# A two-layer transformer block on one core: a finer first attention and a later last recurrence

## The chip, the core and the metric

The kernel runs on one core of a Trainium2 chip. The core has five engines with an instruction list each: TensorE (PE) for products, VectorE (DVE) for elementwise work, reductions and scans, ScalarE (ACT) for functions and copies with a scale, GpSimd (POOL), here mostly for issuing transfers that add into SBUF, and SyncE (SP) for plain transfers. A list is worked off strictly in order; engines wait for each other by semaphores. The metric is the device time of one execution in microseconds, lower is better.

## The reference

Two layers, each of an attention and a feed-forward part, on `x` of shape (4, 256, 256), that is 4 batches of 256 tokens and 256 channels. Each of the four parts is fed not with `x` itself but with `x` gated by a bidirectional recurrence over `fside`:

```python
decay = exp(-exp(w)) * (0.5 + 0.5 * tf);  ek = exp(min(kf, 30));  ekv = ek * vf
# forwards and backwards over time: a = a * decay + ekv_t;  b = b * decay + ek_t
num = nf + nb - ekv + exp(min(u + kf, 30)) * vf
den = df + db - ek + exp(min(u + kf, 30))
out = sigmoid(r) * num / max(den, 1e-8) * (0.8 + 0.2 * tf)      # r is x
```

First attention: `w = x @ W.T` in 16 heads of 16; `q`, `k`, `v` are `w` normalised by its root mean square in each head, times the gains `g1`, `g2`, `g3`. The weights are `softmax(att, -1) + softmax(att, -2)`, and the output goes through `W`. First feed-forward: one product with both sides in 8 bits, scaled by the largest value of the whole input. Second attention: `q`, `k` rotated by position, blocks masked causally, softmax over rows. Second feed-forward: two products with ternary weights and activations rounded to 8 bits, a squared ReLU between them. After each part `x = x + part`.

## The kernel before

The recurrences are independent of `x`, so they are run ahead. There are 16, numbered `n = 4 * part + batch`. Each needs, in this order: `prepare(n)` on ACT (two exponentials and the decay tile), `inputs(n)` on DVE, two forward scans `ahead(n, 0)` and `ahead(n, 1)`, two backward scans `behind(n, 0)` and `behind(n, 1)`, the adding transfers `add_mid(n)` and `add_back(n)` issued by POOL, `wkv(n)` on ACT (a logarithm and an exponential, which give the reciprocal), and `gate(n)` on DVE. Then `gated(part, batch)` multiplies the gate with `1 + tanh(x / 2)` of `tanh(part, batch)`. Recurrence 0 is summed by DVE itself (`summed`).

The first attention is written as 38 slots `p`, eight for each batch (`b, j = divmod(p, 8)`), two heads a slot. In each slot every engine's list holds its share of: scores of slot `p` (`scores0`), their exponential (L486), every second slot the values (`values0`), copy and turn of their rows (`rows_copy`, `turn_rows`), the division `links` on DVE, which also yields scaled values for the column softmax, and the column product (`columns0`). For the next batch a slot holds in turn: projection `project0` (j = 1), `square0` and `sums0` (2), `rms` (3), `normed` (4), transposes of the rows by `turn` (5), `kT_copy` (6) and `low_parts` (7), which split keys and queries into two half-precision parts. `v_rows` on POOL multiplies the values with `g3`. Behind comes the output of the batch before: `turn_y`, `yT_copy`, `turned_copy`, `project_both`, `residual`. Recurrence `n` from 3 on is placed by `M_AT[n] = 3 * (n - 3)`: `prepare` one slot before, `inputs` at it, scans one and two behind, `wkv` five, `gate` six.

After the slots come the tail with recurrence 15's scans, `wkv(13)` and `wkv(14)`, the largest value, the 8-bit product and its scaled copy (L515), bias and sum (L840, L842), `gated(2, 0)`.

The second attention has slots from -16 (`SLOTS1`). At slots -16, -8, 0, 8 it holds `gated(2, b)`, `project_qk` (L1139) and the rotation `rotary`, then `project_v` and POOL's additions (L338), the turns of q and k (L996), copies, `maxima` on PE and `negmax` (L865) on DVE 11 slots ahead of their use, a second turn of q with the maxima in it, and from slot 0 on `scores1`. `wkv(LAST)` stands at slot -4, its gate at 0. PSUM tile `PM` of two banks serves all projections and turns.

## Time and profile before

| | us |
|---|---|
| median of 3 runs | 414.3 (413.16 to 419.51) |
| the profiled execution | 414.29 |
| its span | 412.5 |
| PE busy in it | 270.0 (65%) |
| DVE busy | 264.5 (64%) |
| ACT busy | 203.1 (49%) |
| POOL busy | 53.9 (13%) |

The span is the part that the profiler records on the core. Busy shares are means over stages that have different limits, so none of them says by itself what an edit is worth.

### The profile page before, as it was taken

How to read it: one execution, taken by the hardware profiler on the slowest of the kernel's cores; microseconds unless marked ns; L12 is line 12 of the kernel's file. 1: busy time of each engine (PE TensorE's matmuls, PEld its weight loads, DVE VectorE, ACT ScalarE, POOL GpSimd, SP SyncE). 2: the span in 40 equal slices, each digit the busy share in tenths (PEclk: the TensorE clock that was granted, in tenths of full speed). 3: DMA queues.
4: the chain of work that ended last, by engine and by line, in shares of the span. 5: the costliest groups of instructions: out<-in, count | busy, mean ns of one | idle time of the engine just before them, and what ended most of it. 6: DMA issues, size and time to landing. Idle time of an engine off the chain costs nothing.

```text
span 412.5 us, 5473 instructions
## 1 busy us (share of the span) xinstructions
PE 270.0 (65%) x2054; PEld 165.7 (40%) x2054; DVE 264.5 (64%) x494; ACT 203.1 (49%) x326; POOL 53.9 (13%) x79
## 2 busy tenths in 40 slices
PE   0031564769388498683266867789899899665644
PEld 0020422436145245252132444546666666334413
DVE  4695996987688786799743746373464230694762
ACT  4744369574775854648212272734542533143521
POOL 3012031131013022121330203020000000000000
PEclk9975589598598778867585859998965955966986
DMA  7825255264266355455200000000000000000100
GB/s 202 318 52 102 51 104 102 52 117 88 52 172 126 61 104 114 91 102 102 53 0 0 0 2 0 2 0 2 2 1 2 0 2 0 2 0 0 52 27 25
DMA packets 8522, 23.55 MB, mean 57 GB/s; under 512 B 1584, under 2 KB 2992, under 8 KB 8112
## 3 DMA queue, kind: packets, MB, share of 16 engines
q0 software_dynamic: 4320, 15.73, 20.2%
q1 hardware_dynamic: 4176, 7.48, 5.4%
...
## 4 chain that ended last, share of the span: by engine, by line
PE 41%; DVE 24%; ACT 17%; issue 9%; DMA 5%; SPq 1%; POOL 1%; DVEq 0%; ACTq 0%; POOLq 0%
PE PS L1191 8%; PE PM L1139 5%; PE PM L996 4%; PE PO L1206 3%; DVE fwd L639 3%; PE PO L1042 3%; PE PO L1027 3%; PE PM L1082 3%; PE PM L1068 2%; DVE fwd L910 2%; DMA fwd<-bwd 2%; DVE bwd L647 2%; PE PO L1270 2%; DMA fwd<-mid 2%; ACT E L486 2%
## 5 line engine op out<-in xcount | busy, mean ns | idle before, releaser
L865 DVE TENSOR_REDUCE kp<-PS 128x2 f32<-128x256 f32 x64 | 32.3, 553 | 34.6 <-PE PS L1170 34.6
L486 ACT ACTIVATE E<-PS,negc,escale 128x1024 f32<-128x1024 f32 x32 | 38.3, 1199 | 15.1 <-PE PS L1010 15.1
L554 ACT ACTIVATE E<-PS 128x384 f32<-128x384 f32 x64 | 27.9, 490 | 35.0 <-PE PS L1191 35.0
L1042 PE MATMUL PO<-E,vr 128*32 128x256 f32 x256 | 23.7, 502 | 22.2 <-DVE vr L748 16.4
L1010 PE MATMUL PS<-TP 32*128 32x256 f16 x256 | 21.8, 303 | 22.5 <-DVE TP L689 22.5
L996 PE MATMUL PM<-ident,kp 128*128 128x128 f32 x128 | 21.6, 323 | 11.1 <-DVE kp L677 6.4
L1139 PE MATMUL PM<-G,sg 128*128 128x512 f32 x32 | 20.8, 809 | 9.4 <-DVE sg L662 9.3
L984 PE MATMUL PM<-w,sg 128*128 128x256 f32 x32 | 11.2, 511 | 23.2 <-DVE sg L662 23.2
L458 ACT ACTIVATE yc<-PO 128x256 f32<-128x256 f32 x32 | 12.4, 386 | 25.6 <-PE PO L1027 24.2
L267 POOL DMA_DIRECT2D fwd<-mid x15 | 13.8, 918 | 85.5 <-DVE fwd L639 85.5
L1010 PEld LDWEIGHTS PS<-TP 32*128 32x128 f16 x256 | 10.7, 101 | 33.8 <-DVE TP L689 23.6
L1191 PE MATMUL PS<-TP 32*128 32x128 f32 (+1 forms) x128 | 20.4, 419 | 5.7 <-ACT E L554 3.2
L1027 PE MATMUL PO<-E,vt 128*32 128x256 f32 x256 | 23.7, 501 | 0.0
L996 PEld LDWEIGHTS PM<-ident,kp 128*128 128x128 f32 x128 | 17.1, 165 | 14.8 <-issue 8.3
L1191 PE MATMUL PS<-w,TP 32*128 32x256 f32 (+1 forms) x128 | 20.4, 428 | 2.6 <-ACT E L554 2.5
...
L1042 PEld LDWEIGHTS PO<-E,vr 128*32 128x32 f32 x256 | 8.2, 128 | 31.2 <-DVE vr L748 22.4
L639 DVE TENSOR_TENSOR_SCAN fwd<-DT,ekv 128x512 f32<-128x512 f32 x16 | 20.3, 1267 | 0.0
L647 DVE TENSOR_TENSOR_SCAN bwd<-ekv,DT 128x511 f32<-128x511 f32 x16 | 20.2, 1262 | 0.0
L1191 PEld LDWEIGHTS PS<-TP 32*128 32x128 f32 x128 | 15.2, 230 | 12.0 <-ACT E L554 4.4
L639 DVE TENSOR_TENSOR_SCAN fwd<-DT,ek 128x512 f32<-128x512 f32 x16 | 19.5, 1217 | 0.0
L386 ACT ACTIVATE fwd<-fwd,lnmin 128x512 f32<-128x512 f32 x16 | 11.5, 721 | 15.9 <-DMA fwd<-bwd 15.9
...
## 6 DMA issues: line engine op xcount, KB each, us to landing
fwd<-mid POOLq DMA_DIRECT2D x15, 512.0 KB, 4.6
fwd<-bwd POOLq DMA_DIRECT2D x15, 512.0 KB, 4.5
...
w<-in_attn SPq DMA_DIRECT2D x1, 512.0 KB, 7.1
```

The costliest lines, as they stand in the source:

```text
L267: nc.gpsimd.dma_start(fwd[:, r], mid[:, o], accum_op=ALU.add).then_inc(S[f"mid_added{o}"], 16)
L486: nc.scalar.activation(E[:, p % 6], PS[:, 2 * (p % 2):2 * (p % 2) + 2, :], ACT.Exp, bias=negc[:], scale=escale[:]).then_inc(S["e0_done"], 1)
L554: nc.scalar.activation(E[:, p % 4, i, 0:384], PS[:, i, 0:384], ACT.Exp, scale=QSCALE).then_inc(S["e1_done"], 1)
L639: nc.vector.tensor_tensor_scan(fwd[:, r, i], DT[n % 2][:, 0:SEG], src[:, seg(b)], 0.0, ALU.mult, ALU.add).then_inc(S["scan_done"], 1)
L647: nc.vector.tensor_tensor_scan(bwd[:, n % 2, i, 0:SEG - 1][:, ::-1], src[:, seg(b, 1, SEG - 1)][:, ::-1], DT[n % 2][:, 1:SEG][:, ::-1], 0. ...
L865: nc.vector.tensor_reduce(kp[:, b % 2, u * H + 2 * j:u * H + 2 * j + 2, D], PS[:, at0:at0 + 2, lo:hi], AX, ALU.max, negate=True).then_inc( ...
L996: ins = nc.tensor.transpose(PM[:, c // 2, at:at + P], src.rearrange("p g s -> p (g s)"), ident[:])
L1010: ins = nc.tensor.matmul(PS[:, 2 * (p % 2) + i, u * T:(u + 1) * T], khl[b % 2][r:r + SLOT, c, u * P:(u + 1) * P], q[b % 2][r:r + SLOT, c, ...
L1027: ins = nc.tensor.matmul(PO[SLOT * g:SLOT * (g + 1), 0, 0:T], vt[:, b % 2, v * H + 4 * c + g, :], E[:, (2 * q + g // 2) % 6, g % 2, v * T: ...
L1042: ins = nc.tensor.matmul(PO[SLOT * g:SLOT * (g + 1), 1, at:at + T], vr[:, q % 2, v * 4 + g, :], E[:, (2 * q + g // 2) % 6, g % 2, v * T:(v ...
L1139: ins = nc.tensor.matmul(PM[:, u, :], sg[:, seg(b, k * T + u * P, P)], w1a[:, k, 0:2, :].rearrange("p n c -> p (n c)"), start=(k == 0), st ...
L1191: ins = nc.tensor.matmul(PS[:, i, 2 * v * P:2 * P + v * P], k[r:r + ROWS, c, v * P:(v + 1) * P], q[r:r + ROWS, c, v * P:2 * P], start=True ...
```

## The change

- Key chain in halves. The transposes of a batch (`turn`) become `turn0(b, k)`: half `k` (two of the four head groups) in slots 5 and 6, with `kT_copy(b, k)` and `low_parts(b, k)` in halves as well; `scores0` waits for the half that it reads. A transpose of 128 columns becomes four products with 32 columns each.
- Values in place. `normed` writes both copies of a row into a wider tile `kv`, whose third part holds ones; `values0` and `links` read the values there. `v_rows` and its semaphore go. `g3` is applied in the scale of `yT_copy` and `turned_copy`.
- First logarithm moved up. Loads are reordered (`x` first), all four `tanh(0, s)` stand behind `prepare(0)`, and `wkv(0)` stands before `prepare(1)`.
- Recurrences: `n = 2` leaves the head for slot 0, so that 2 to 11 are spread over slots 0 to 33, `n = 12` takes the place of 15 in the tail, and 13 to 15 go to the slots -15 to -2 of the second attention, with `wkv(12)` and `gate(12)` at the first of them.
- Order in a slot: on ACT `wkv` stands behind the exponential and the copies, on DVE `residual` stands first and `low_parts` behind the scans. `gated(2, 0)` and its tanh stand behind the second residual sum of the feed-forward; the weight steps move by one slot.

```diff
-        kp = sb("kp", [P, 2, 2 * TT * H, SLOT])
+        kpf = sb("kp", [P, 2 * 2 * TT * H * SLOT])
+        kp = kpf[:].rearrange("p (n r s) -> p n r s", n=2, s=SLOT)
+        WIDE = 3 * D
+        kv = kpf[:, 0:2 * TT * H * WIDE].rearrange("p (n r s) -> p n r s", n=2, s=WIDE)
...
-        RAMP = 3
+        RAMP = 2
+        BEFORE = 3 * LAYERS
         LAST = LAYERS * B - 1
-        M_AT = {n: 3 * (n - RAMP) for n in range(RAMP, LAYERS * B)}
-
+        M_AT = {n: 3 * (n - RAMP) for n in range(RAMP, BEFORE)}
+        M_AT[BEFORE] = B * PAIRS + 4
+        M_LATE = {BEFORE + i: -17 + 3 * i for i in range(1, B)}
+
+        def steps1(p, lag):
+            return [n for n, at in M_LATE.items() if at + lag == p]
...
-            sp.dma_start(xT[:, seg(0)], xT_d[:, seg(0)]).then_inc(S["ld_x0"], 16)
+            for b in range(2):
+                sp.dma_start(xT[:, seg(b)], xT_d[:, seg(b)]).then_inc(S[f"ld_x{b}"], 16)
+            sp.dma_start(gcol[:], gcol_d).then_inc(S["ld_gcol"], 16)
+            sp.dma_start(gains[:], gains_d.partition_broadcast(P)).then_inc(S["ld_gains"], 16)
             sp.dma_start(kT[:, seg(1)], kT_d[:, seg(1)]).then_inc(S["ld_k1"], 16)
-            sp.dma_start(w0[:], attn0_d).then_inc(S["ld_attn0"], 16)
-            sp.dma_start(kT[:, seg(2)], kT_d[:, seg(2)]).then_inc(S["ld_k2"], 16)
-            sp.dma_start(gains[:], gains_d.partition_broadcast(P)).then_inc(S["ld_gains"], 16)
-            sp.dma_start(gcol[:], gcol_d).then_inc(S["ld_gcol"], 16)
-            sp.dma_start(ident[:], ident_d).then_inc(S["ld_ident"], 16)
-            sp.dma_start(xT[:, seg(1)], xT_d[:, seg(1)]).then_inc(S["ld_x1"], 16)
-            sp.dma_start(kT[:, seg(3)], kT_d[:, seg(3)]).then_inc(S["ld_k3"], 16)
             for b in range(2, B):
                 sp.dma_start(xT[:, seg(b)], xT_d[:, seg(b)]).then_inc(S[f"ld_x{b}"], 16)
+            sp.dma_start(w0[:], attn0_d).then_inc(S["ld_attn0"], 16)
+            sp.dma_start(ident[:], ident_d).then_inc(S["ld_ident"], 16)
+            for b in range(2, B):
+                sp.dma_start(kT[:, seg(b)], kT_d[:, seg(b)]).then_inc(S[f"ld_k{b}"], 16)
...
-            def v_rows(b):
-
-                pool.wait_ge(S["k0_done"], b + 1)
-                if b >= 2:
-                    pool.wait_ge(S["pv0_done"], CH * (b - 1))
-                nc.gpsimd.tensor_tensor(vt[:, b % 2, :, 0:D], kp[:, b % 2, 0:TT * H, 0:D],
-                                        gains[:, 2, None, :].broadcast_to([P, TT * H, D]),
-                                        ALU.mult).then_inc(S["v0_done"], 1)
...
+            nc.gpsimd.memset(kv[:, :, :, 2 * D:WIDE], 1.0).then_inc(S["pads_set"], 1)
...
+            add_mid(1)
+            add_back(1)
+            for p in range(SLOTS0):
+                for n in steps0(p, 1):
+                    if n < BEFORE:
+                        add_mid(n)
+                for n in steps0(p, 2):
+                    if n < BEFORE:
+                        add_back(n)
+            add_mid(BEFORE)
+
+
+            pool.wait_ge(S["ktr0_done"], HALF * B)
+            pool.wait_ge(S["y0_done"], B * CH)
             nc.gpsimd.memset(vt[:, :, :, D:2 * D], 1.0).then_inc(S["v_ones"], 1)
...
+            add_back(BEFORE)
             for p in SLOTS1:
                 b, j = p // PAIRS + 2, p % PAIRS
+                for n in steps1(p, 1):
+                    add_mid(n)
+                for n in steps1(p, 2):
+                    add_back(n)
...
+                    for s in range(B):
+                        tanh(0, s)
                 if b == 1:
-                    tanh(0, 0)
-            prepare(1)
-            for b in range(1, B):
-                tanh(0, b)
-            nc.scalar.preload_act_table_set("natural_log_exp_and_others")
-            act.wait_ge(S["ln_bias"], 1)
-            wkv(0)
-            prepare(2)
+                    nc.scalar.preload_act_table_set("natural_log_exp_and_others")
+                    act.wait_ge(S["ln_bias"], 1)
+                    wkv(0)
+                    prepare(1)
...
-            def kT_copy(b):
-                act.wait_ge(S["ktr0_done"], b + 1)
+            def kT_copy(b, k):
+                act.wait_ge(S["ktr0_done"], HALF * b + k + 1)
                 if b >= 2:
-                    act.wait_ge(S["qk0_done"], PAIRS * (b - 1))
-                rows = PM[:].rearrange("p k (c t) -> p (k c) t", t=T)
-                nc.scalar.activation(khigh[b % 2], rows, ACT.Copy).then_inc(S["kT0_done"], 1)
-                nc.scalar.activation(qhigh[b % 2], rows, ACT.Copy, scale=gq[:]).then_inc(S["kT0_done"], 1)
-
-            def yT_copy(b, turned, used, done):
+                    act.wait_ge(S["qk0_done"], PAIRS * (b - 2) + 4 * k + 4)
+                rows = PM[:, k, :].rearrange("p (c t) -> p c t", t=T)
+                nc.scalar.activation(khigh[b % 2][:, 2 * k:2 * k + 2], rows, ACT.Copy).then_inc(S["kT0_done"], 1)
+                nc.scalar.activation(qhigh[b % 2][:, 2 * k:2 * k + 2], rows, ACT.Copy,
+                                     scale=gq[:]).then_inc(S["kT0_done"], 1)
...
             square0(0)
+            prepare(2)
+            rms(0)
             weight_abs(0)
-            rms(0)
-            weight_abs(1)
             act.wait_ge(S["gains_done"], 1)
-            wkv(1)
-            kT_copy(0)
-            prepare(3)
+            for k in range(HALF):
+                kT_copy(0, k)
             for p in range(SLOTS0):
                 b, j = divmod(p, PAIRS)
-                if p == 2:
-                    wkv(2)
-                for n in steps0(p, 5):
-                    if n <= 12:
-                        wkv(n)
                 if p < B * PAIRS:
...
-                if p % 2 == 0 and 0 <= p // 2 - 1 < B * CH:
-                    rows_copy(p // 2 - 1, 0, "pv0_done", "turned0_done", "rows0_done")
-                if j == 2 and b + 1 < B:
+                if p == 0:
+                    wkv(1)
+                    weight_abs(1)
+                if j == 1 and b + 1 < B:
                     square0(b + 1)
                 if j == 3 and b + 1 < B:
                     rms(b + 1)
+                if p % 2 == 0 and 0 <= p // 2 - 1 < B * CH:
+                    rows_copy(p // 2 - 1, 0, "pv0_done", "turned0_done", "rows0_done")
                 if j == 3 and 1 <= b <= B:
-                    yT_copy(b - 1, "ytr0_done", "out0_done", "yT0_done")
+                    yT_copy(b - 1, "ytr0_done", "out0_done", "yT0_done", gv[:])
+                if j == 5 and b + 1 < B:
+                    kT_copy(b + 1, 0)
+                if j == 6 and b + 1 < B:
+                    kT_copy(b + 1, 1)
                 if p % 4 == 3 and p >= 7 and (p - 7) // 4 < B * HALF:
                     turned_copy((p - 7) // 4)
-                if j == 6 and b + 1 < B:
-                    kT_copy(b + 1)
+                for n in steps0(p, 5):
+                    if n < BEFORE:
+                        wkv(n)
                 for n in steps0(p, -1):
                     if n > RAMP:
                         prepare(n)
-                if p in (5, 13):
-                    weight_round(1 - (p - 5) // 8)
+                if p in (4, 12):
+                    weight_round(1 - (p - 4) // 8)
                 if p == 33:
                     for bb in range(B - 1):
                         tanh(1, bb)
 
 
             tanh(1, B - 1)
-            for n in range(13, LAST):
-                wkv(n)
             for b in range(B):
                 act.wait_ge(S["ffn0_done"], b + 1)
                 nc.scalar.activation(y8[:, b], PS[:, b, :], ACT.Copy, scale=sc8[:, 5:6]).then_inc(S["y8_done"], 1)
+                if b == 1:
+                    tanh(2, 0)
 
...
-                if p == -4:
-                    wkv(LAST)
+                for n in steps1(p, -1):
+                    prepare(n)
+                if steps1(p, 5):
+                    nc.scalar.preload_act_table_set("natural_log_exp_and_others")
+                for n in steps1(p, 5):
+                    if n == BEFORE + 1:
+                        wkv(BEFORE)
+                    wkv(n)
...
             inputs(1)
+            sums0(0)
             ahead(1, 0)
+            normed(0)
             ahead(1, 1)
-            sums0(0)
             behind(1, 0)
+            low_parts(0, 0)
             behind(1, 1)
-            normed(0)
-            inputs(2)
-            ahead(2, 0)
-            ahead(2, 1)
-            low_parts(0)
-            behind(2, 0)
-            behind(2, 1)
-            gate(1)
+            low_parts(0, 1)
...
-                if j == 0 and b + 1 < B:
-                    gated(0, b + 1)
+                if j == 5 and 1 <= b <= B:
+                    residual("out0_done", b, 0, b - 1)
                 if j == 4 and b + 1 < B:
                     normed(b + 1)
-                if j == 7 and b + 1 < B:
-                    low_parts(b + 1)
-                if p == 3:
-                    gate(2)
-                for n in steps0(p, 6):
-                    if n <= 12:
-                        gate(n)
-                if p == SLOTS0 - 2:
-                    for bb in range(B - 1):
-                        gated(1, bb)
-                        largest(bb)
                 for n in steps0(p, 0):
                     inputs(n)
                 for n in steps0(p, 1):
-                    if n < LAST:
+                    if n < BEFORE:
                         ahead(n, 0)
                         ahead(n, 1)
                 for n in steps0(p, 2):
-                    behind(n, 0)
-                    behind(n, 1)
-                if j == 5 and 1 <= b <= B:
-                    residual("out0_done", b, 0, b - 1)
+                    if n < BEFORE:
+                        behind(n, 0)
+                        behind(n, 1)
+                if p == 0:
+                    gate(1)
+                for n in steps0(p, 6):
+                    if n < BEFORE:
+                        gate(n)
+                if j == 0 and b + 1 < B:
+                    gated(0, b + 1)
+                if j == 6 and b + 1 < B:
+                    low_parts(b + 1, 0)
+                if j == 7 and b + 1 < B:
+                    low_parts(b + 1, 1)
                 if p % 2 == 1 and 0 <= (p - 3) // 2 < B * CH:
                     links((p - 3) // 2)
                 if j == 2 and b + 1 < B:
                     sums0(b + 1)
+                if p == 34:
+                    for bb in range(B - 1):
+                        gated(1, bb)
+                        largest(bb)
                 if p == 1:
...
-            behind(LAST, 0)
-            behind(LAST, 1)
+            behind(BEFORE, 0)
             for b in range(B):
                 dve.wait_ge(S["y8_done"], b + 1)
...
                 nc.vector.tensor_tensor(xT[:, seg(b)], xT[:, seg(b)], y8[:, b], ALU.add).then_inc(S["x_done"], 1)
+                if b == 1:
+                    gated(2, 0)
+            behind(BEFORE, 1)
...
-                if p in (-15, -13, 0):
-                    gate(13 + (p + 15) // 2 if p < 0 else LAST)
+                for n in steps1(p, 6):
+                    if n == BEFORE + 1:
+                        gate(BEFORE)
+                    gate(n)
+                for n in steps1(p, 0):
+                    inputs(n)
+                for n in steps1(p, 1):
+                    ahead(n, 0)
+                    ahead(n, 1)
+                for n in steps1(p, 2):
+                    behind(n, 0)
...
+            def turn0(b, k):
+                if k == 0:
+                    pe.wait_ge(S["k0_done"], b + 1)
+                elif b >= 2:
+                    pe.wait_ge(S["x_done"], b - 1)
+                for c in (2 * k, 2 * k + 1):
+                    for u in range(TT):
+                        at = (c % 2) * T + u * P
+                        for g in range(4):
+                            ins = nc.tensor.matmul(PM[SLOT * g:SLOT * (g + 1), k, at:at + P],
+                                                   kv[:, b % 2, u * H + 4 * c + g, 0:SLOT], ident[:],
+                                                   start=True, stop=True)
+                ins.then_inc(S["ktr0_done"], 1)
...
                 if j == 5 and b + 1 < B:
-                    turn(b + 1, 0, "ktr0_done", [("k0_done", b + 2)] + ([("x_done", b)] if b >= 1 else []))
+                    turn0(b + 1, 0)
+                if j == 6 and b + 1 < B:
+                    turn0(b + 1, 1)
```

## Rows read from the trace of the kernel before

**Rows 1.** Stretches: start:end us, length, busy us (instructions) by engine, granted clock, DMA share, GB/s.

```profile
74.29:110.19 35.90, 25.14 (x236) 14.73 (x236) 27.95 (x41) 22.79 (x34) 7.29 (x7) 0.79 0.47 89
...
167.70:189.85 22.15, 12.77 (x72) 7.39 (x72) 19.83 (x31) 12.18 (x21) 3.44 (x4) 0.77 0.50 95
...
204.13:243.25 39.12, 27.20 (x117) 14.68 (x117) 19.19 (x37) 12.52 (x15) 6.72 (x10) 0.67 0.00 0
243.25:412.50 169.25, 131.79 (x972) 86.22 (x972) 81.39 (x209) 65.67 (x121) 6.16 (x9) 0.79 0.02 7
```

**Rows 2.** Head, timeline: start, length, engine, line, tiles, count, [idle before <-releaser].

```profile
18.69 0.69 DVE L613 SCALAR_TENSOR_TENSOR G<-fwd 128x512 f32<-128x512 f32 x1 [3.04 <-ACT fwd L388]
...
20.23 3.46 PE L984 MATMUL PM<-w,sg 128*128 128x256 f32 x8 [20.23 <-DVE sg L662]
...
36.73 0.72 ACT L386 ACTIVATE fwd<-fwd,lnmin 128x512 f32<-128x512 f32 x1 [7.66 <-DMA fwd<-bwd]
...
42.60 1.07 PE L1010 MATMUL PS<-TP 32*128 32x256 f16 x16 [10.53 <-DVE TP L689]
...
51.56 1.21 ACT L486 ACTIVATE E<-PS,negc,escale 128x1024 f32<-128x1024 f32 x1 [0.30 <-PE PS L1010]
```

**Rows 3.** The page's table of groups: busy us and mean ns of one, idle before.

```profile
L865 DVE TENSOR_REDUCE kp<-PS 128x2 f32<-128x256 f32 x64 | 32.3, 553 | 34.6 <-PE PS L1170 34.6
...
L639 DVE TENSOR_TENSOR_SCAN fwd<-DT,ekv 128x512 f32<-128x512 f32 x16 | 20.3, 1267 | 0.0
...
L386 ACT ACTIVATE fwd<-fwd,lnmin 128x512 f32<-128x512 f32 x16 | 11.5, 721 | 15.9 <-DMA fwd<-bwd 15.9
```

**Rows 4.** First attention, timeline.

```profile
57.97 1.93 PE L1042 MATMUL PO<-E,vr 128*32 128x256 f32 x16 [3.89 <-DVE vr L748]
...
60.36 2.24 DVE L639 TENSOR_TENSOR_SCAN fwd<-DT,ekv 128x512 f32<-128x512 f32 x1
...
83.45 1.07 PE L1042 MATMUL PO<-E,vr 128*32 128x256 f32 x16
...
106.58 1.28 DVE L687 SCALAR_TENSOR_TENSOR TP<-TP,gcol,PM 128x1024 f16<-128x1024 f16 x1 [4.35 <-ACT TP L444]
...
163.40 0.69 DVE L694 TENSOR_TENSOR xT<-PM,xT 128x512 f32<-128x512 f32 x1 [3.41 <-PE PM L1082]
...
174.80 0.43 DVE L626 TENSOR_SCALAR mid<-mid 128x512 f32<-128x512 f32 x1 [1.90 <-ACT mid L369]
```

**Rows 5.** The page's DMA issues: median us from issue to landing, last.

```profile
fwd<-mid POOLq DMA_DIRECT2D x15, 512.0 KB, 4.6
fwd<-bwd POOLq DMA_DIRECT2D x15, 512.0 KB, 4.5
```

**Rows 6.** End of the first attention and first feed-forward, timeline.

```profile
186.49 0.68 DVE L694 TENSOR_TENSOR xT<-PM,xT 128x512 f32<-128x512 f32 x1
...
192.29 3.57 PE L1124 MATMUL PS<-E,w8q 128*128 128x256 fp8e4 x16 [1.94 <-DVE E L833]
...
195.70 2.40 ACT L515 ACTIVATE E<-PS,cond 128x512 bf16<-128x512 f32 x4
...
203.39 0.68 DVE L662 SCALAR_TENSOR_TENSOR sg<-sg,G 128x512 f32<-128x512 f32 x1
```

**Rows 7.** From 204.13 us to the second attention, timeline.

```profile
211.60 0.60 ACT L564 ACTIVATE vt<-PM 128x512 f32<-128x512 f32 x1 [12.98 <-PE PM L1148]
...
219.68 0.63 ACT L359 ACTIVATE sg<-xT 128x512 f32<-128x512 f32 x1
...
223.01 6.18 PE L1139 MATMUL PM<-G,sg 128*128 128x512 f32 x8 [1.03 <-DVE sg L662]
...
230.91 1.41 POOL L338 TENSOR_TENSOR kp<-G 128x256 f32<-128x256 f32 x2 [0.92 <-DVE G L854]
...
232.38 1.10 PE L996 MATMUL PM<-ident,kp 128*128 128x128 f32 x8 [0.22 <-POOL kp L338]
...
238.32 1.28 ACT L386 ACT_TABLE_LOAD   x1
```

88 lines of the change are left out of this document (37 added, 51 removed).

## The prediction

> **What bounds the kernel now.** I first cut the span into stages by the table of stretches [rows 1], then read each stage in order of time for who waits for whom. The table of groups gives the price of one operation. No engine is full anywhere: in the first attention the VectorE (DVE) is busy 27.95 of 35.90 us per batch and the TensorE (PE) 25.14, between the attentions DVE is busy 19.19 of 39.12. What costs time is that each engine runs its own list in order, and a list stands still whenever its head waits. So I don't compare sums of work. I carry the new lists through, with the durations of the rows, and note when each list is at the same point. "Slot" is the index of the written order, S(n) a pair of scans of recurrence n, log(n) the two ScalarE (ACT) operations of `wkv(n)`.
>
> Three places matter. The head: the first scores start at 42.60, after PE idled 10.53 [rows 2], and one ScalarE operation on 512 columns costs 0.72 there [rows 3]. The first attention: DVE idles 4.35 at the low parts of the keys, which comes once a batch, and 3.41 at a residual [rows 4]. The stretch 204.13 to 243.25, from the projection of q and k of batch 0 to the first scores of the second attention [rows 1]: a chain PE, DVE, GpSimd (POOL), PE, ACT, DVE in which every engine idles and none may be late.
>
> **Head.** DVE waits 3.04 us for log(0) [rows 2]. In the new order ACT has log(0) done before the numerator is summed, so the gate starts 3.0 earlier and the projection at 17.2 instead of 20.23. It ends at 20.7 (3.46 us, [rows 2]). Then square 0.6, head sums 0.65, an interposed `prepare(2)` of 1.5 (two exponentials of 256 columns and a copy of 510, two and a half times the 0.6 to 0.7 of 512 columns, [rows 3]), root 0.55: 23.4. Two normalising operations 1.25, first half of the turn 1.8, two copies of 512 columns 1.1, two low parts 1.3: first scores near 29, 13.5 earlier. The full-width turn before took 1.94 with PE at 1.2 GHz; the new one is 16 products per half, 32 columns wide. Its nearest row is the column product: 8 such products (16 instructions) with 256 moving columns, four to side-by-side quarters of the output, show as 1.93 at 1.2 GHz and 1.07 at 2.4 [rows 4]. 16 products with 128 columns move as many columns, so I take the same, 1.0 to 1.9. Bounds per half: below, the old turn's 1.94 for both halves, 0.5 each at 2.4 GHz; above, if the four don't overlap, four times 1.93, 7.7.
>
> Most is not kept. After exponential 0, ACT has log(1), which needs the second accumulating transfer: S ends at 25.8 and 30.1, the transfers take 4.6 and 4.5 to land [rows 5] plus 0.5 to start, so log(1) starts at 35.4, behind it stand the sum of the second weight and exponential 1 (39), gate 1, the gating of batch 1 and its projection (38.2 to 41.9). Exponential 2 comes at 43.5, against 51.56 [rows 2]: **-8.1**.
>
> **Slots 2 to 31.** Density of recurrences is the same, one per three slots, one index behind. Gone: the POOL multiplication for the values, beside which a scan of 1.2 took 2.24 [rows 4]; one wait of 4 us per batch shrinks because half 0 of the keys is ready when DVE gets there. New: the inputs of n wait on DVE for `prepare(n)`, which stands behind log, copies and exponential on ACT. This wait exists now (1.90 before the inputs at 174.80, [rows 4]); in my walk it is 2.5 to 3 at slots 6, 9, 15 and more at 18. Also new: the residual is first in its slot instead of behind the scans, so DVE stands before it for 3 us while scans could run (now: 3.41, in one batch only, [rows 4]). And logs move behind the exponential of their slot, which takes the transfer's wait off the exponentials. Checkpoints of the walk, against now: exponential 8 -11.6, 16 -10.3, 24 -7.8. I enter **-2** for this stage (bounds +4 and -8).
>
> **Slots 28 to 38.** Recurrences 13 and 14 leave, and 12 shrinks to its inputs and one scan: 18 us of DVE work (6.3 per recurrence: four scans, 1.13 apart in order of time though 1.22 each [rows 3], inputs 0.43 + 0.7 [rows 4], gate 0.69 [rows 2]). I credit only **-1**. The 22.15 us after the last exponential [rows 1] are bound by exponential, columns, values, copy, turn, and PE's two projections; DVE's work lay in their gaps. It was late at the end only for the last residual, which stands behind the inputs of 15 and starts at 186.49 [rows 6]; PE was done about 1 us before. In front of the links of the last quarter the new order even puts gate 11, which waits for log(11).
>
> **First feed-forward.** Products start at 192.29, the first scaled copy only at 195.70, since log(13) and log(14) with four table loads lie before it [rows 6]: -2.5. The gating of batch 0 moves from behind all four residual sums (203.39, [rows 6]) to behind the second: two sums of some 1.2 (estimate: two operations of 0.3 and one of 0.7) and a scan of 1.13, which moves behind them, less what POOL's clearing of `kp` (now right behind transfer 12) blocks of the first sum: -2.3. Together **-4.8**. The scan behind and two sums fit under PE's 3.8 us until the first rotation. So the projection starts at 204.1 - 8.1 - 2 - 1 - 4.8 = 188.
>
> **The stretch to the second attention.** Times from that start; now it ends at 39.1 [rows 1]. Recurrences 13, 14, 15 enter.
> (a) ACT: the copy of v ends at 8.1 [rows 7], `prepare(13)` 9.6; DVE inputs 10.2, S(13) ahead 12.45. POOL 0.5, transfer 4.8 to the next issue, second one 4.5: log(13) can start at 22.3. Behind it in ACT's list is the tanh of batch 1, which now starts at 15.6 (219.68, [rows 7]). 22.3 + log 1.35 + table load 1.28 + tanh 0.63 + gating 0.7 = 26.3, and q, k of batch 1 are projected then, instead of 18.9: **+7.4**. DVE, with three maxima and four scans, is ready at about the same time, so both would have to be faster.
> (b) POOL: the list puts transfer 15 ahead of the rotary additions of batch 1. It needs S(15) ahead, and this stands behind both rotations. From the projection's start: rotations done 7.8, two gates 1.25, inputs 1.1, a pair of maxima 1.0 (0.55 each, [rows 3]), scans 2.3, issue 0.5 + 0.9, additions twice 1.4 [rows 7], clearing 0.15: turn of q at 17.9, now 9.4 (223.01 to 232.38, [rows 7]): **+8.5**.
> (c) Turn of q to first scores, now 10.9: log(15) with two loads, 4.0 from 238.32 [rows 7], goes from in front of the copy of q. Enter: turn and copy 2.2, load and log(14) 2.6, gate 14 0.6 in front of maxima 6 and 7 (1.9), turn 2.0, copy 1.0, log(15) 2.6 (1.35 if the set, still loaded, isn't loaded again), gate 15 0.6 in front of maxima 9 and 10 (1.9), for which the first scores wait: 15.5. **+4.6**.
> Gate 15 is gone from the second attention, -0.6. Sum +19.9; bounds: +12, if the waits of (c) fall into the lag of (b) and the third load is absent, and +24.
>
> The Trainium skill speaks against this placement (ScalarE: Activation LUTs, What ACT_TABLE_LOAD costs): it puts a switch of set at about 2.66 us, drain included. The load here takes 1.28 [rows 7]. By the page three switches on the chain would add some 4 us to the sum.
>
> **Sum.** The rest, 169.25 us [rows 1], has the same lists and stays. 412.5 - 16 + 20 = 416.5 of span; the profiled execution took 414.29, 1.8 more than its span and equal to the median of 414.3. Forecast **418**. Its own range is 411 to 424.
>
> **Rivals.** (1) The first attention is bound by DVE after all. Then what leaves counts in full: 18.7 us, and the contention of 3, on top of the head. For it: DVE is busy 78% of the batch [rows 1], more than any other. Against it: PE has 70%, in other places of the slot, and each waits for the other. The projection would start 27 earlier instead of 16: 407. (2) The stretch absorbs the recurrences, as DVE is idle for 19.93 of 39.12 there. Then only the excess of DVE's list over the chain stays, about 6: 404. Against it: (a) is a transfer latency and (b) an order on one queue; neither asks how idle DVE is. (3) Slower: DVE's stands in front of the residual. At slots 13, 21 and 29 the residual waits for PE's projection; now the scans run in that wait. If each of the three costs its full 3.3 on the links behind it, the first part gains only 6: 426.5 + 1.8 = 428. It decides if the links of slots 13, 21, 29 come over 2.6 us after the residual; a pair of scans stands between only at 29, which speaks against the full price. (4) The head doesn't move: x of batches 2 and 3 now load before the second key segment and ACT's tanh of them stands before log(0). If they land after 12.7, log(0) is as late as now: 3 back, 421.
>
> **Chances.** Forecast 0.47, (1) 0.15, (2) 0.13, (3) 0.20, (4) 0.05. A measurement of this kernel tells 2% from no change, 406.0 and 422.6. Faster: (2) and a third of (1), with some of my walk's own error, 0.20. Slower: (3) and the upper end of the forecast, 0.27. Range 403 to 427: from under (2) to just short of (3), where the ends of the unknown costs (-24 + 12 and -8 + 24 on the span) lie as well.
>
> **What would show it.** First scores near 29 and exponential 2 near 43.5; an ACT wait of some 4 us before log(1). Exponentials 8, 16, 24 at -11, -10, -8. Start of the q, k projection near 188. Then table load, log(13), load, tanh in ACT's order with a wait on the transfer, 26 us from that start to the second projection; POOL's additions of batch 1 behind a transfer issue; DVE waiting for ACT before gates 14 and 15; some 59 us to the first scores. Wrong if the stretch is under 50, or if the projection starts before 180.

## The result, and the profile after

The changed kernel takes **429.75 us** (median of 3 runs, 429.28 to 430.33) against 414.3: ratio 1.0388, 95% interval 1.0343 to 1.0434. The forecast was 418.0, range 403 to 427: right in sign, 11.75 us short, and outside the range. The profiled execution is that of the median: 429.75, span 428.0, mean granted clock 0.780.

I put the marks of the two traces side by side, each the start of the same work, and beside them the mark of the forecast.

| us | before | forecast | after |
|---|---|---|---|
| exponential 2 | 51.56 | 43.5 | 46.48 |
| exponential 24 | 142.9 | 135.1 | 135.5 |
| exponential 31 | 167.7 | | 164.6 |
| 8-bit quantisation | 191.65 | | 185.40 |
| 8-bit products | 192.29 | | 189.69 |
| projection q, k of batch 0 | 204.13 | 188 | 195.01 |
| of batch 1, from there | +18.9 | +26.3 | +26.50 |
| turn of q of batch 1, from there | +9.4 | +17.9 | +18.83 |
| first scores, from there | +10.9 | +15.5 | +16.82 |
| end, from there | 169.25 | 168.65 | 170.8 |

By its terms the forecast's span ends at 416.4 (188 + 59.7 + 168.65). Of the 11.6 us that it is longer, 7.0 are there when the projection starts, 2.4 come in the stretch and 2.2 behind the first scores. The table of stretches has the same three places (start:end, length, busy us of PE, weight load, DVE, ACT, POOL, granted clock, DMA share, GB/s); its rows answer to [rows 1]:

```profile
63.70:101.50 37.80, 25.17 (x292) 15.08 (x292) 29.39 (x46) 24.64 (x39) 5.15 (x6) 0.82 0.42 79
164.60:185.40 20.80, 11.61 (x74) 7.35 (x74) 12.31 (x26) 9.13 (x15) 0.13 (x1) 0.83 0.01 1
195.01:257.16 62.15, 28.47 (x117) 15.83 (x117) 40.59 (x65) 25.14 (x33) 13.14 (x18) 0.61 0.31 59
257.16:427.90 170.74, 132.66 (x972) 86.53 (x972) 80.55 (x208) 65.24 (x120) 5.79 (x9) 0.79 0.02 7
```

DVE's work in the stretch between the attentions doubles, 19.19 to 40.59, while its length grows by 23.0.

**Head.** ACT's timeline, answering to [rows 2]:

```profile
7.22 0.21 ACT L398 ACTIVATE ew<-vec 128x8 f32<-128x8 f32 x1 [1.92 <-DMA vec<-in_vec]
...
38.54 0.72 ACT L389 ACTIVATE fwd<-fwd,lnmin 128x512 f32<-128x512 f32 x1 [4.52 <-DMA fwd<-bwd]
...
46.48 1.20 ACT L482 ACTIVATE E<-PS,negc,escale 128x1024 f32<-128x1024 f32 x1 [0.56 <-PE PS L1042]
```

The wait in front of log(1) is there, 4.52 for "some 4". The first scores start at 32.15 (forecast: near 29). Everything is shifted: the first small load is used at 7.22, in before's trace at 4.76.

**Last batch of the first attention.** DVE's timeline:

```profile
150.87 1.20 DVE L649 TENSOR_TENSOR_SCAN fwd<-DT,ekv 128x512 f32<-128x512 f32 x1
157.29 0.69 DVE L704 TENSOR_TENSOR xT<-PM,xT 128x512 f32<-128x512 f32 x1 [5.21 <-PE PM L1112]
157.89 1.21 DVE L657 TENSOR_TENSOR_SCAN bwd<-ek,DT 128x511 f32<-128x511 f32 x1
159.02 1.20 DVE L657 TENSOR_TENSOR_SCAN bwd<-ekv,DT 128x511 f32<-128x511 f32 x1
160.13 0.18 DVE L744 RECIPROCAL rrec<-PO 128x8 f32<-128x8 f32 x1
```

The two scans behind the residual don't need it. They stand still with it for 5.21 us, and the links (the reciprocal) come behind both, 2.84 behind the residual. At slots 13 and 21 it is much the same: waits of 3.49 and 3.53 us, and the links 2.86 and 2.33 behind. On the page the residual's row (8 of them, four in the first attention) has the idle time in front:

```profile
L704 DVE TENSOR_TENSOR xT<-PM,xT 128x512 f32<-128x512 f32 x8 | 5.5, 690 | 26.9 <-PE PM L1112 15.0
```

The 15.0 us are the four of the first attention (3.49, 3.53, 5.21, 2.74); in the trace before they are 5.6.

**First feed-forward.** DVE, then POOL, then the 8-bit products on PE:

```profile
185.40 5.36 DVE L839 TENSOR_SCALAR E<-sg,cond 128x512 fp8e4<-128x512 f32 x4
```

```profile
185.27 0.86 POOL L276 DMA_DIRECT2D fwd<-mid  x1 [23.64 <-DVE fwd L649]
185.80 1.71 POOL L316 MEMSET vt<- 128x1536 f32 x1
187.12 2.14 POOL L319 MEMSET kp<- 128x2048 f32 x1
```

```profile
189.69 3.57 PE L1157 MATMUL PS<-E,w8q 128*128 128x256 fp8e4 x16 [5.60 <-DVE E L839]
```

Four quantisations took 1.68 in all before; they take 5.36 here, of which the first alone has 4.15: it ends at 189.55, just behind the large fills (189.26). The products wait for it and start 4.29 us behind its start, 0.64 before. In the trace before, the fill of `kp` lay beside the second pair of bias sums, which took 2.60 instead of 0.61:

```profile
197.65 2.60 DVE L840 TENSOR_SCALAR E<-E,bias 128x256 bf16<-128x256 bf16 x2
...
197.71 2.14 POOL L321 MEMSET kp<- 128x2048 f32 x1
```

**The stretch.** Logarithm 13 on ACT, which waits for its transfer until 22.4 from the start (forecast 22.3) and stands ahead of the tanh of batch 1; POOL's issue of transfer 15 ahead of the additions; and DVE's two waits for gates:

```profile
217.41 0.72 ACT L389 ACTIVATE fwd<-fwd,lnmin 128x512 f32<-128x512 f32 x1 [0.69 <-DMA fwd<-bwd]
...
220.11 0.63 ACT L362 ACTIVATE sg<-xT 128x512 f32<-128x512 f32 x1
```

```profile
235.31 0.86 POOL L276 DMA_DIRECT2D fwd<-mid  x1 [13.79 <-DVE fwd L649]
...
236.42 3.86 POOL L341 TENSOR_TENSOR kp<-G 128x256 f32<-128x256 f32 x4
```

```profile
246.09 0.69 DVE L623 SCALAR_TENSOR_TENSOR G<-fwd 128x512 f32<-128x512 f32 x1 [6.77 <-ACT fwd L391]
...
254.46 0.69 DVE L623 SCALAR_TENSOR_TENSOR G<-fwd 128x512 f32<-128x512 f32 x1 [4.88 <-ACT fwd L391]
```

### The profile page after: what moved, and what is told of

Read it like the earlier page. It is cut to its first block, busy times and chain, and to the rows that moved or that the text cites. A ratio compares the mean times of both kernels' runs of the same rounds, so it can differ in the third digit from the quotient of the medians.

```text
span 428.0 us, 5935 instructions
## 1 busy us (share of the span) xinstructions
PE 275.2 (64%) x2278; PEld 170.7 (40%) x2278; DVE 262.7 (61%) x502; ACT 204.8 (48%) x333; POOL 47.1 (11%) x76
## 4 chain that ended last, share of the span: by engine, by line
PE 44%; DVE 27%; ACT 12%; issue 10%; DMA 4%; POOL 2%; DVEq 0%; ACTq 0%; POOLq 0%
PE PS L1224 7%; DVE fwd L649 5%; PE PO L1072 5%; PE PM L1172 4%; PE PM L1112 4%; PE PO L1057 4%; PE PO L1239 3%; PE PM L1028 3%; PE PM L1098 2%; DVE fwd L918 2%; DMA fwd<-mid 2%; DMA fwd<-bwd 2%; DVE bwd L657 2%; PE PM L1181 2%; DVE kp L873 2%
## 5 line engine op out<-in xcount | busy, mean ns | idle before, releaser
L873 DVE TENSOR_REDUCE kp<-PS 128x2 f32<-128x256 f32 x64 | 32.3, 551 | 25.5 <-PE PS L1203 25.4
L482 ACT ACTIVATE E<-PS,negc,escale 128x1024 f32<-128x1024 f32 x32 | 38.3, 1198 | 11.6 <-PE PS L1042 11.4
L1072 PE MATMUL PO<-E,vr 128*32 128x256 f32 x256 | 22.7, 483 | 32.7 <-DVE vr L751 26.4
L460 ACT ACTIVATE yc<-PO 128x256 f32<-128x256 f32 x32 | 12.4, 387 | 30.5 <-PE PO L1057 29.1
L1224 PE MATMUL PS<-TP 32*128 32x256 f32 (+1 forms) x128 | 20.2, 417 | 9.3 <-DVE kp L873 6.0
L1172 PE MATMUL PM<-G,sg 128*128 128x512 f32 x32 | 21.8, 842 | 6.6 <-DVE sg L672 6.5
L1028 PE MATMUL PM<-ident,kp 128*128 128x128 f32 x96 | 17.5, 341 | 10.9 <-POOL kp L341 8.8
L1057 PE MATMUL PO<-E,kp 128*32 128x256 f32 x256 | 23.2, 494 | 0.0
L623 DVE SCALAR_TENSOR_TENSOR G<-fwd 128x512 f32<-128x512 f32 x16 | 10.9, 686 | 18.5 <-ACT fwd L391 18.3
L1203 PE MATMUL PS<-E 32*128 32x128 bf16 (+1 forms) x128 | 12.1, 292 | 15.5 <-DVE kp L873 14.4
L704 DVE TENSOR_TENSOR xT<-PM,xT 128x512 f32<-128x512 f32 x8 | 5.5, 690 | 26.9 <-PE PM L1112 15.0
L1002 PEld LDWEIGHTS PM<-w,sg 128*128 128x128 f32 x32 | 7.9, 261 | 30.1 <-DVE sg L672 28.7
```

The costliest lines, as they stand in the source:

```text
L482: nc.scalar.activation(E[:, p % 6], PS[:, 2 * (p % 2):2 * (p % 2) + 2, :], ACT.Exp, bias=negc[:], scale=escale[:]).then_inc(S["e0_done"], 1)
L873: nc.vector.tensor_reduce(kp[:, b % 2, u * H + 2 * j:u * H + 2 * j + 2, D], PS[:, at0:at0 + 2, lo:hi], AX, ALU.max, negate=True).then_inc( ...
L1002: ins = nc.tensor.matmul(PM[:, 0, u * C:(u + 1) * C], sg[:, seg(b, k * T + u * P, P)], w0[:, 0, k, :], start=(k == 0), stop=(k == HALF - 1))
L1028: ins = nc.tensor.transpose(PM[:, c // 2, at:at + P], src.rearrange("p g s -> p (g s)"), ident[:])
L1057: ins = nc.tensor.matmul(PO[SLOT * g:SLOT * (g + 1), 0, 0:T], kv[:, b % 2, v * H + 4 * c + g, D:WIDE], E[:, (2 * q + g // 2) % 6, g % 2, v ...
L1072: ins = nc.tensor.matmul(PO[SLOT * g:SLOT * (g + 1), 1, at:at + T], vr[:, q % 2, v * 4 + g, :], E[:, (2 * q + g // 2) % 6, g % 2, v * T:(v ...
```

## The experiments

Sixteen kernels ran in four groups, each group on one chip beside runs of the kernel before (414.71, 414.54, 414.63 and 416.09 us there). "Projection" below is the start of q, k of batch 0, "rest" the time from the first scores to the end of the span, "clock" the granted TensorE clock. The medians of the kernel before differ by up to 1.5 us between the groups, so small differences across groups are better read from the ratios. The first small load is issued at 1.65 in every trace, but is used at 4.50 to 5.03 in the four traces without late recurrences (before, e7, e9, e13) and at 5.78 to 7.22 in the fourteen with them. Marks of two traces can differ by up to 2.7 us from that alone, and why it goes with the kernel, the runs don't show.

### The two halves of the change

**e4, the kernel before with recurrences 13 to 15 moved to the second attention, and nothing else.**

```
-        M_AT = {n: 3 * (n - RAMP) for n in range(RAMP, LAYERS * B)}
+        BEFORE = 3 * LAYERS
+        M_AT = {n: 3 * (n - RAMP) for n in range(RAMP, BEFORE)}
+        M_AT[BEFORE] = B * PAIRS + 4
+        M_LATE = {BEFORE + i: -17 + 3 * i for i in range(1, B)}
...
```

> The kernel before with the late recurrences alone: 12 in the tail, 13 to 15 in the slots before the second attention, as in the changed kernel; head, keys, values and orders of the first attention as before. If the late placement is the loss, the stretch is 60 to 62 us instead of 39 and the end of the first attention gains 2 to 5: before plus 17 to 21, 431 to 435 us. If the loss is in the finer first attention, the time is near 414 to 418.

429.72 us, ratio 1.0381 (1.033 to 1.0431): the whole loss comes with them alone. Their logarithms, gates, scans and transfers stand as in the changed kernel. The quantisation starts at 184.91 instead of 191.65 though the last exponential isn't earlier (168.3), so the recurrences that leave free 7.3 us between the two, where I had entered 1. The stretch takes 63.4 us instead of 39.1.

**e7, the changed first attention with all 16 recurrences in it.**

```
-        M_AT[BEFORE] = B * PAIRS + 4
-        M_LATE = {BEFORE + i: -17 + 3 * i for i in range(1, B)}
+        M_AT[13], M_AT[14], M_AT[LAST] = 32, 34, B * PAIRS + 4
...
```

> The changed first attention (keys in halves, values in place, logarithm and loads moved) with all 16 recurrences in it and their logarithms and gates placed as before; 13 to 15 start at slots 32, 34 and 36. No recurrence in the second attention. Theory A (all of the loss is the late recurrences, +15 us by the run of before with them alone, and the first attention's own changes are worth about nothing): 413 to 416, projection of q and k at 203 to 206. Rival (the head's 8 to 11 us are real and are kept until the end of the first attention when VectorE's list is short enough): projection at 196 to 199 and 406 to 409 us.

412.54 us, ratio 0.9945 (0.9899 to 0.9992). Here the first load was used at 4.50, and exponential 2 came at 43.3, where the forecast had it. The projection starts at 199.04, 5.1 earlier than before: less than half of the 11.9 by which exponential 16 is (98.3 against 110.2). The time lies between the two that I had expected to choose from. The first attention's own change is worth 0.5%, and late recurrences on top of it cost 17.2.

### The end of the first attention

**e12, the residual behind the scans of its slot again.**

```
-                if j == 5 and 1 <= b <= B:
-                    residual("out0_done", b, 0, b - 1)
...
+                if j == 5 and 1 <= b <= B:
+                    residual("out0_done", b, 0, b - 1)
                 if p % 2 == 1 and 0 <= (p - 3) // 2 < B * CH:
                     links((p - 3) // 2)
```

> The changed kernel with one part undone: the residual of the first attention stands behind the scans of its slot again, in front of the links. Rival (3) of my prediction said that the residual in front lets VectorE wait with scans behind it; the trace has that wait, 5.21 us at 157.29. If it costs: the last exponential comes 2 to 4 us earlier and the time is 426 to 428. If not (the links have time): within 0.7 us of 429.75.

421.10 us (419.73 to 422.37), **8.65 less** than the changed kernel and more than expected; ratio to before 1.0162 (1.0093 to 1.023). DVE's timeline at the same place:

```profile
148.21 1.19 DVE L657 TENSOR_TENSOR_SCAN bwd<-ek,DT 128x511 f32<-128x511 f32 x1
149.32 1.19 DVE L657 TENSOR_TENSOR_SCAN bwd<-ekv,DT 128x511 f32<-128x511 f32 x1
153.51 0.69 DVE L704 TENSOR_TENSOR xT<-PM,xT 128x512 f32<-128x512 f32 x1 [3.00 <-PE PM L1112]
154.43 0.21 DVE L744 RECIPROCAL rrec<-PO 128x8 f32<-128x8 f32 x1 [0.22 <-PE PO L1081]
```

The scans run in the wait, and the links come 0.92 behind the residual instead of 2.84. That is 1.9 us of order at this place. The four waits of the first attention come to 5.4 us instead of 15.0. The table of stretches, from exponential 24 to 31 and on to the quantisation, of the changed kernel and then of e12, shows where more of it lies:

```profile
135.50:164.60 29.10, 23.93 (x211) 12.53 (x204) 15.54 (x25) 14.37 (x21) 4.09 (x5) 0.73 0.48 91
```

```profile
133.60:157.80 24.20, 20.45 (x194) 11.19 (x186) 15.44 (x25) 14.15 (x21) 3.44 (x4) 0.79 0.58 110
157.80:177.07 19.27, 10.30 (x74) 6.29 (x74) 12.31 (x26) 9.14 (x16) 0.13 (x1) 0.85 0.00 1
```

The first stretch is 4.9 us shorter. Of that, 1.9 lie already between exponentials 24 and 25 (139.90 less 135.52, against 136.06 less 133.62), where no residual stands; PE waits longer there for the links and its next two groups of products take longer. The changed kernel, then e12:

```profile
135.25 1.93 PE L1072 MATMUL PO<-E,vr 128*32 128x256 f32 x16 [3.37 <-DVE vr L751]
...
136.95 1.93 PE L1057 MATMUL PO<-E,kp 128*32 128x256 f32 x16
```

```profile
132.49 1.07 PE L1072 MATMUL PO<-E,vr 128*32 128x256 f32 x16 [2.60 <-DVE vr L751]
...
133.38 1.66 PE L1057 MATMUL PO<-E,kp 128*32 128x256 f32 x16
```

The other 3.0 lie between exponentials 29 and 31, around the residual. The clock is granted at 0.79 instead of 0.73, and at 0.85 instead of 0.83 behind the last exponential; the two projections there took 5.8 us (3.78 and 2.19, overlapping) in the changed kernel and 3.7 (1.99 and 1.89) in e12, the same 16 products. This is no accident of one run: of the kernels with the residual in front, eleven traces have 29.1 to 30.1 us from exponential 24 to 31, and e8 has 28.0; with it behind the scans it is 23.6 to 25.5 in e12, e13, e14, e15 and in both kernels of the old order (before, e4). So the order costs, and a lower clock comes with it (0.9 us between these two traces are the head's). How the 8.65 divide between the two, and whether the clock follows from the order alone, the runs don't separate.

**e6, POOL's clearing moved.**

```
             nc.gpsimd.memset(kv[:, :, :, 2 * D:WIDE], 1.0).then_inc(S["pads_set"], 1)
+            nc.gpsimd.memset(vt[:, :, :, D:2 * D], 1.0).then_inc(S["v_ones"], 1)
...
             pool.wait_ge(S["y0_done"], B * CH)
-            nc.gpsimd.memset(vt[:, :, :, D:2 * D], 1.0).then_inc(S["v_ones"], 1)
+            pool.wait_ge(S["xq8_done"], B)
```

> The changed kernel with only GpSimd's clearing moved: the ones beside the values of the second attention are set at the start, and kp is cleared after the four 8-bit quantisations instead of beside them. Theory A (the clearing stretches the quantisation, which took 5.36 us instead of 1.68): the quantisation takes 1.7 again, the 8-bit products and the projection of q and k start 3.7 earlier, and the time falls by 3 to 4 us to about 426. Rival (the clearing costs the same wherever it lies, since VectorE's bias sums are then stretched): the products start 3.7 earlier, the projection by under 1, and the time stays within 1 us of 429.7.

425.09 us (422.93 to 425.51), **4.7 less**; ratio to before 1.0249 (1.0178 to 1.032). DVE, then POOL:

```profile
184.15 1.68 DVE L840 TENSOR_SCALAR E<-sg,cond 128x512 fp8e4<-128x512 f32 x4
...
186.87 1.31 DVE L846 TENSOR_SCALAR E<-E,bias 128x256 bf16<-128x256 bf16 x2
```

```profile
185.97 1.81 POOL L320 MEMSET kp<- 128x2048 f32 x1 [0.86 <-DVE E L840]
```

The quantisation is back at 1.68, 3.7 less, and 2.95 of that arrive at the projection: the interval from quantisation to projection falls from 9.61 to 6.66. The other 0.7 go to the first pair of bias sums, beside which the fill now lies: 1.31 instead of 0.58. (The projection itself is 4.2 earlier, 1.2 of it from the head.)

**e8, the two halves of the keys handled together.**

```
-                if j == 5 and b + 1 < B:
+                if j == 6 and b + 1 < B:
                     turn0(b + 1, 0)
...
```

ACT's copies of half 0 go from 5 to 6 and DVE's low parts from 6 to 7.

> The changed kernel with one part undone: in the loop of the first attention the two halves of the keys are turned, copied and split together at the slots of the second half (6, 6 and 7), as a whole. Theory A (halving takes one wait of some 4 us per batch down, as my prediction had it within its -2): exponentials 8, 16 and 24 later by 1 to 3 each, in all 2 to 5 us at the projection, 432 to 434 us. Rival (the halves gain nothing, since PE and VectorE wait elsewhere in the slot): exponentials within 0.5 us of the changed kernel, 429 to 431 us.

429.76 us, equal to the changed kernel, where I had expected 432 to 434 if the halves were worth anything. Exponentials 8 and 16 come 2.8 and 2.2 later (66.5, 103.7), 24 is 1.8 later, 31 only 0.7, and the projection 0.7. The halves work as described, and their gain is given back before the attention ends.

### The stretch

**e1, POOL's additions of batch 1 ahead of the transfers.**

```
             for p in SLOTS1:
-                for n in steps1(p, 1):
-                    add_mid(n)
-                for n in steps1(p, 2):
-                    add_back(n)
...
                                                     ALU.add).then_inc(S["qkp_done"], 1)
+                for n in steps1(p, 1):
+                    add_mid(n)
+                for n in steps1(p, 2):
+                    add_back(n)
```

> The changed kernel (429.75 us) with one order altered: on GpSimd the rotary additions of batch 1 stand ahead of the issue of recurrence 15's first transfer. If the additions' place in that queue is a link of the chain, the turn of q of batch 1 starts some 9 us after its projection instead of 18.8, and, as VectorE then still has scans and a gate ahead of maxima 6 and 7, the stretch to the second attention shrinks from 62 to 52 to 55 us: 420 to 423 us. If the stretch is bound by VectorE's own list (recurrences 13 to 15 and the gates in it), less than 2 us are gained: 428 to 430.

423.11 us (421.18 to 425.14), **6.6 less**; the turn of q of batch 1 is 13.0 behind its projection instead of 18.8, and the stretch is 56.0, a little more than the 52 to 55 expected.

**e2, gates 12 and 13 at slot -8, gates 14 and 15 at slot 3 of the second attention.**

```
-                for n in steps1(p, 6):
-                    if n == BEFORE + 1:
-                        gate(BEFORE)
-                    gate(n)
+                if p == -8:
+                    gate(BEFORE)
+                    gate(BEFORE + 1)
...
+                if p == 3:
+                    gate(BEFORE + 2)
+                    gate(BEFORE + 3)
```

> The changed kernel with gates 14 and 15 behind slot 3 of the second attention instead of slots -5 and -2. The changed trace shows VectorE idle 6.8 us before gate 14 and 4.9 before gate 15. If these stands are the cost, the first scores come 5.6 earlier and the first exponential, which stands behind log 15 and a tanh on ScalarE, 3 earlier: 426 to 427.5 us. If the maxima behind gate 14 wait for the turn of q anyway and those behind gate 15 for ScalarE's logarithm in another way, nothing changes: 429 to 430.

Three executions took 429.34 to 430.69 and one 416.21, with the granted clock at 0.761 to 0.780 and 0.826, so no ratio is given. The profiled one, of clock 0.761, has the stretch 4.7 shorter (57.4) and the rest 4.4 longer (175.3). With such a spread neither expectation is settled.

**e3, both, and the logarithms moved**: 12 and 13 behind the tanh of batch 1, 14 and 15 to slot 2.

```
-                if steps1(p, 5):
+                if p in (-8, 2):
                     nc.scalar.preload_act_table_set("natural_log_exp_and_others")
...
```

> The changed kernel with the stretch reordered as a whole: additions first on GpSimd, logs 12 and 13 behind the tanh of batch 1, logs 14 and 15 at slot 2, gates 14 and 15 at slot 3. If the recurrences cost time there only by where they stand in the lists, the stretch falls from 62 to some 45 us and the kernel to 411 to 415. If VectorE's added 19 us of work or the transfers bound the stretch, it stays at 52 or more: 420 us or more.

421.22 us (419.06 to 423.47), ratio 1.0162 (1.0116 to 1.0208). The stretch falls to 48.4, 7.6 under e1, and only 1.9 of that are in the time: the rest takes 178.25 instead of 170.8. The stretch came near the 45 expected, the time (411 to 415) didn't.

### All together

**e9 and e13: e7 with e6's clearing, then with e12's residual besides.**

> As the kernel with the changed first attention alone (e7), and GpSimd's clearing moved as in e6. Theory A: 3 to 4 us under e7, so about 410 to 412. Rival: equal to e7.

> No late recurrences: the changed first attention alone (e7) with the clearing moved (e9) and the residual behind the scans (e12). If all three add up: 412.5 less 3 to 5 less 0 to 3, so 406 to 410 and faster than before by 1 to 2%. Rival (the first attention gives a shift of its own back in the granted clock, as e9 did against e7): 411 to 413.

e9: 412.02 us, four executions from 403.76 to 415.37 with clocks of 0.773 to 0.834; its exponential 31 came 3.0 later than in e7, and the gain of the clearing can't be read from it. e13: **408.17 us** (402.82 to 408.5), ratio 0.9829 (0.9751 to 0.9907). This is the version that beats both kernels: the new first attention, the old stage for the recurrences, the old place of the residual, and the clearing behind the quantisation.

**e10, e11, e14, e15: the late recurrences kept, mended.** e14 is e1, e6 and e12; e15 is e3, e6 and e12; e10 is e3 and e6; e11 is e10 with logarithms 14, 15 at slot 9 and gates at 10.

> The changed kernel, its late recurrences kept, with three orders mended: the residual behind the scans (e12, -8.6), the clearing moved (e6, -4.7), GpSimd's additions of batch 1 ahead of the transfer (e1, -6.6). If the three add up: 409.8, so under before (414.6), and within 2 us of e13, which has no late recurrences (408.2); then nothing of the loss lies in the recurrences themselves. Rival (they overlap, or the stretch waits on the transfer latency of recurrence 13 anyway): 413 to 418.

> e14 with the logarithms and gates of e3 besides (12 and 13 behind the tanh, 14 and 15 at slots 2 and 3 of the second attention): the stretch 7 us shorter. If that is kept: 403 to 405. Rival (as in e3 and e10, the second attention takes 7 to 10 us longer for it): 408 to 411, as e14.

> The changed kernel with the late recurrences kept and all mends together: the edits of e3 (GpSimd's additions ahead of the transfers, logarithms 12 and 13 behind the tanh, logarithms 14 and 15 at slot 2, gates at slots -8 and 3) and the clearing moved as in e6. If the mends add up: 421.2 less 4.7, about 416.5, still no faster than before. Rival (what e3 lost behind the first scores, where its second attention took 178.25 us and not 170.8, depends on the granted clock and not on the logarithms in it): anywhere from 409 to 420, with a second attention of 170 to 178.

> As e10, but logarithms 14 and 15 stand at slot 9 of the second attention and gates 14 and 15 at slot 10. Theory A (the two logarithms and two table loads, 5.2 us of ScalarE, hold the exponentials wherever they stand inside the attention): the same as e10 within 1 us. Theory B (at slots 2 and 3 they hold the copies and the projection of q and k of batch 3, which stood at +34.0 instead of +29.5 us behind the first scores; at slot 9 they meet idle ScalarE): second attention 3 to 7 us shorter than in e10, and 410 to 413 us.

| | us (range) | ratio to before | stretch | rest |
|---|---|---|---|---|
| e14 | 412.25 (411.17 to 417.19) | 0.995 (0.9909 to 0.9991) | 55.8 | 170.4 |
| e15 | 415.11 (411.57 to 416.78) | 0.9996 (0.9957 to 1.0035) | 48.5 | 181.3 |
| e10 | 419.96 (417.15 to 422.91) | 1.0145 (1.007 to 1.022) | 48.7 | 181.0 |
| e11 | 421.49 (419.16 to 424.12) | 1.0183 (1.0112 to 1.0254) | 50.2 | 175.3 |

Three orders, 8.65 + 4.7 + 6.6 = 20.0 alone, are worth 17.5 together, between the two expectations: e14 has the three late recurrences and loses nothing to before. It isn't free of them, though: e13, without them, stands 1.2% lower by the two ratios. Their ledger in these two traces: the projection starts at 185.05 against 195.51 (10.5 gained), the stretch takes 55.8 against 38.7 (17.1 lost). The further mends of e3, e10, e11 and e15 shorten the stretch by 6 to 8 (against e1 or e14) and lose most of it or more behind the first scores. So three expectations failed: e10 (416.5), e15 (403 to 411), and e11, whose rest is 5.6 us shorter than e10's, as theory B had it, while its time isn't.

### Where the rest gives it back

**e16 and e17: e10 with pure delay ahead of the first scores.**

```
+                if p == -2:
+                    for _ in range(8):
+                        link(nc.vector.memset(otile[:], 0.0))
...
```

e17 has 16 of them.

> e10, whose second attention took 180.9 us, with eight chained fills of 128x512 on VectorE at slot -2, just ahead of the first scores: pure delay, some 3 to 5 us. Theory A (the logarithms and gates at slots 2 and 3 make the second attention long): the first scores and the end are both later by the delay, 423 to 425 us. Theory B (the granted clock falls at other places of the same list when the list is shifted, and that makes 170 or 181 of it): the rest behind the first scores changes by several us in either direction; the end is not later by the delay.

> The same with sixteen fills, 6 to 10 us. Theory A: 426 to 430 us. Theory B: less than that, with a second attention nearer to 171 us, whose first scores then lie where the slower kernels have them.

e16: 421.96 us (419.48 to 427.37), e17: 429.26 (422.67 to 430.19). The fills took 5.1 and 10.4, and the stretch is 2.9 and 8.9 longer than in e10 (48.69). The rest behind the first scores, for the changed kernel (above, 170.74), e10, e16 and e17:

```profile
240.05:421.00 180.95, 140.13 (x972) 91.13 (x972) 82.14 (x210) 70.67 (x127) 5.77 (x9) 0.75 0.02 7
```

```profile
244.24:417.80 173.56, 133.68 (x972) 87.08 (x972) 81.69 (x210) 70.36 (x126) 5.78 (x9) 0.79 0.02 7
```

```profile
248.81:427.90 179.09, 138.69 (x972) 90.37 (x972) 81.87 (x210) 70.28 (x126) 5.77 (x9) 0.76 0.02 7
```

The last three run one list of instructions there, 972 matmuls each, and take 173.6 to 181.0. The difference is mostly PE's own busy time (133.68, 138.69, 140.13), at clocks of 0.79, 0.76, 0.75: 6.5 of the 7.4 us between e10 and e16. So 7.4 us of e10's rest aren't the logarithms and gates, which e16 has as well; at most 2.8 (173.56 less 170.74) are theirs, if e16's clock is taken for undisturbed. The profiled e16, delayed by 5.1 us, ended 3.2 earlier than the profiled e10, but that was the longest of e10's four executions and nearly the shortest of e16's. By the medians theory B isn't clear-cut: e16 is 2.0 over e10 (0.2% by the ratios to before), e17 9.3 (1.3%). What decides the pattern of the clock, the runs don't show. All seven profiled kernels with late recurrences and all logarithms ahead of the first scores have 170.2 to 173.0; all seven with logarithms or gates behind them have 173.6 to 181.3. Single executions stand behind these figures; those of e2, e10 and e17 are among the long ones of their kernels.

## Why the prediction was wrong

Of the 16 us that the projection was to start earlier, the trace has 9.1. The head gives 5.1 (forecast 8.1). From exponential 2 to 31 the changed kernel loses 2.0 (forecast: gains 2). From there to the quantisation it gains 3.1 (forecast 1), and from there to the projection 2.9 (forecast 4.8).

**The head: right but for its start.** Exponential 2 was forecast at 43.5, came at 46.48 in the trace after and at 43.3 where the first load was used as early as in before's trace. Of the missing 3.0, 2.5 are the later landing of the first small load, not rival (4): in the trace after, gate 0 starts at 18.22 without a wait for log(0). My error was to add a saving to marks of one execution as if the loads landed there in the new kernel too.

**Slots 2 to 24: near, in part by luck.** Exponentials 8, 16, 24 came 10.6, 8.7 and 7.4 earlier (forecast 11.6, 10.3, 7.8). With the head 3.0 late that means that slots 2 to 8 gave 2.0 more than my walk had, which hid most of the head's miss.

**"The residual is first in its slot", in the -2 of slots 2 to 31: the step that failed.** Rival (3) was true, on top of the forecast and not in its place. I had weighed it down because "a pair of scans stands between only at 29", priced it by the links it holds up, and gave it 0.20. The reason was wrong: a pair of scans stands between at slot 13 too, and inputs and a gate at 21, so that the links come 2.86, 2.33 and 2.84 behind. The waits are 3.49, 3.53 and 5.21 us, and the order costs 1.9 us at slot 29, but its price by e12 is 8.65; the granted clock from exponential 24 to the quantisation is 0.77 with it and 0.81 without. Where my walk has a gain of 2 us and the trace a loss of 2.0, the loss arises behind exponential 24: from there to exponential 31 it takes 29.1 us, 24.8 before and 24.2 in e12. Without the residual in front the projection starts at 186.7 and the time, 421.10, is inside the range. The measured time is near the 428 of rival (3), but in part by luck, since that sum had the stretch and the feed-forward as forecast and took its 10 us from links alone.

**First feed-forward, -4.8: the size was off.** It gave 2.9. The two savings together gave 6.5, of which 2.0 are the bias sums that the clearing no longer held up, but I had placed the clearing of `kp` beside the first bias sum; it ran beside the quantisation, with the fill of `vt`, and cost 3.7 there. Before the change the ones of `vt` were set in the head, and the clearing of `kp` stood behind the last transfer of recurrence 15. The Trainium skill (SBUF — State Buffer, Who interferes with whom) has the rule that I hadn't applied to this pair: a `tensor_scalar` can go into a mode that uses the port pair shared with GpSimd, and then "the other fully blocks". The trace agrees: 5.36 beside the fills and 1.68 without them, with the first one ending 0.3 us behind the large fills. Which of the two held the ports first doesn't follow from the recorded starts (transfer issue 185.27, quantisation 185.40, fill 185.80).

**Slots 28 to 38, -1: wrong in the other direction.** Taking the recurrences out freed 7.3 us there in e4 and some 10 of the projection between e13 and e14. I had argued from a busy TensorE; with the scans in place DVE reaches the last residual of e7 at 184.26 without any wait, and the scans stand between it and the quantisation. This error hid the two others in part: with residual and clearing mended, e14's projection starts at 185.05 and not at 188.

**The stretch, +19.9: mechanism right.** (a) 26.5 for 26.3, (b) 18.8 for 17.9, (c) 16.8 for 15.5; e1 confirms (b), 5.8 shorter with POOL's order turned. The waits that it named stand in the rows, and log(13) starts at 22.4 for 22.3. Rivals (1) and (2) are out: the stretch didn't absorb the recurrences, though e13 against e14 shows the first attention's end to have been bound by DVE.

**The rest, "has the same lists and stays": true of the lists.** It was 1.6 longer than before, 2.2 longer than forecast, and up to 12 longer in the variants. The forecast had no term for that in its range.

**The range** was also narrower than its own bounds. "-8 + 24 on the span" makes 412.5 + 16 + 1.8 = 430.3, not 427, and would have held the result; the end was drawn just short of rival (3) without a reason for leaving that rival out. In rival (1), "27 earlier" leaves out the contention of 3 that its sentence names.
